# A query front that runs ahead of the first batch's attention, or mixed with it

## The chip, the cores and the metric

The kernel runs on one core of a Trainium2 chip. The metric is the device time of one execution in microseconds (us). A core has a matrix engine (TensorE, PE in the rows; its weight loads are PEld), VectorE (DVE), ScalarE (ACT), GpSimd (POOL) and SyncE (SP), which here only issues transfers (DMAs). Each takes its own list of instructions strictly in order; semaphores join the lists.

## The reference

Three residual blocks over 32 batches of 64 tokens of width 256: cross attention to 1601 context rows, span attention, and a feed-forward block with a shared expert and eight routed ones. Only the first matters here:

```python
def _L0_xattn_ref(q, k, v, mask, wq_w, wq_b, wk_w, wk_b, wv_w, wv_b, wo_w, wo_b):
    qh = _split_heads(q @ wq_w.T + wq_b)          # 16 heads of 16
    kh = _split_heads(k @ wk_w.T + wk_b)
    vh = _split_heads(v @ wv_w.T + wv_b)
    scores = jnp.einsum('bhqd,bhkd->bhqk', qh, kh) / jnp.sqrt(jnp.float32(D_K))
    scores = jnp.where(mask, scores, jnp.float32(-1000000000.0))
    attn = jax.nn.softmax(scores, axis=-1)
    out = jnp.einsum('bhqk,bhkd->bhqd', attn, vh)
    ...
    return out @ wo_w.T + wo_b
x = x + _L0_xattn_ref(_layernorm(x, axis=-1), ctx_1024, ctx_1024, mask, ...)
```

The mask of this case lets every row see every key.

## The kernel before

**Three parts.** `queries` normalizes x and projects the queries of all 2048 tokens, in four chunks of 512. `cross_attention` handles the 32 batches. `tail` is the second part, with span attention and experts; the change leaves it as it is.

**Queries.** A chunk passes: mean by matmul with 1/256 (M), subtraction (C), square (S), variance by matmul (V), ln and exp for the reciprocal deviation (I), the product with it (N, into `xn`), projection by `wq` (P), bias (B), clearing of dead rows (G), split into fp16 high and low parts (H, L). These parts are stored to a buffer in HBM, `q_parts`. `run_periods` sets the order: a period does one step of each kind, for chunks that lie one stage apart. The context of batch 0 is split into high and low parts there too (X, four chunks of 400 columns), and the masks, weights and biases are prepared.

**Between the parts.** `both` emits an engine's share of `queries`, then waits for all that was prepared (`ready`), then the share of `cross_attention`. On PE the latter begins with waits for the constant rows of the key stacks and for the ones in both value tiles, and then reads a register (`rows_all`) and branches: without masked rows it runs one unrolled copy of the loop, otherwise another.

**Cross attention.** A turn works on batch n and prepares batch n+1. In the letters of `SLOTS`: K (eight pieces) projects keys, six matmuls each, which ACT and DVE turn into `k_hi` and `k_lo`; V (thirteen) projects values; SP copies queries and keys into `qstack` and `kstack` (six transfers, and three for each of eight pairs of heads); M (32) is a score matmul whose maximum DVE takes; T turns the row maxima into rows of the query stack; S are the scores for the softmax, P the products with the values. H marks where POOL splits the next context but one into `ctx_hi` and `ctx_lo`; they have one buffer, so chunk i waits until the values of its rows are done. The turn that only prepares, `turn(-1)`, does batch 0's K, V, M and T after the queries.

Of the kernel before, what the change touches and what calls it, by code (L numbers as in the profile page):

```python
# [13 lines left out]
F32 = mybir.dt.float32  # L14
# [89 lines left out]
def build(nc, ins, out_dram):  # L104
    ctx = ExitStack()
    with ctx:
# [9 lines left out]
        wo_in = sem("wo_in")  # L116
# [4 lines left out]
        with ExitStack() as attention:  # L121
            def sb(name, shape, dt):
# [12 lines left out]
                kstack=[sb(f"kstack{i}", [P, PAIRS, S2P], F16) for i in range(2)],  # L135
# [3 lines left out]
                ctx_in=sem("ctx_in"),  # L139
                ctx_hi=sem("ctx_hi"),  # L140
                ctx_lo=sem("ctx_lo"),
                rows_in=sem("select_rows_in"), stack_zero=sem("stack_zero"),
            )
            before, ready = queries(nc, ins, bank, w, first_in, wo, bo, bo_all, wo_in, ident, mean_w, eps_col, q_parts, sem)
            cross = cross_attention(nc, sb, ins, bank, w, first_in, attn_out, out_done, q_parts, sem)
# [32 lines left out]
def run_periods(order, table):  # L178


    depth = max(late for late, _, _ in table.values())
    for period in range(NCH + depth):
        count = {}
        for step in order.split():
            late, do, arg = table[step]
            i = count.get(step, 0)
            count[step] = i + 1
            if 0 <= period - late < NCH:
                do(period - late, i if arg is None else arg)


def queries(nc, ins, bank, w, first_in, wo, bo, bo_all, wo_in, ident, mean_w, eps_col, q_parts, sem):
# [3 lines left out]
    with ExitStack() as own:  # L196
        def sb(name, shape, dt=F32):
# [4 lines left out]
        bq, bk_raw, bq_up = sb("bq", [P, NK]), sb("bk_raw", [P, NK]), sb("bq_up", [P, NK])  # L202
# [7 lines left out]
        sq = [sb(f"sq{i}", [P, NK, CW]) for i in range(2)]  # L210
        rstd = [sb(f"rstd{i}", [P, CW]) for i in range(2)]
        xn = [sb(f"xn{i}", [P, NK, CW]) for i in range(2)]
        q = [sb(f"q{i}", [P, NK, CW]) for i in range(2)]
        q_hi, q_lo = first_in["q_hi"], first_in["q_lo"]
        mean_bank, var_bank, proj_bank, row_bank, bias_bank = bank[0:2], bank[2:4], bank[4:6], bank[6], bank[7]

        x_in = [sem(f"q_x_in{c}") for c in range(NCH)]
        const_in, wq_in, w_in, mask_in = (sem("q_" + n) for n in ("const_in", "wq_in", "w_in", "mask_in"))
        memsets, up_done, parts_hi, consts, rows_seen, diag_ready, live_ready, live_done, bias_sum, bias_done = (
            sem("q_" + n) for n in ("memsets", "up_done", "parts_hi", "consts", "rows_seen", "diag_ready", "live_ready", "live_done",  # L220
                                    "bias_sum", "bias_done"))
        mean, xc_done, sq_done, var, lnv, rstd_done, xn_done, proj, biased, live, hi_done, lo_done = (
            sem("q_" + n) for n in "mean xc sq var lnv rstd xn proj biased live hi lo".split())
        q_out = [sem(f"q_out{i}") for i in range(2)]
        raw, c_hi, c_lo = first_in["raw"], first_in["c_hi"], first_in["c_lo"]

        PE_ORDER, DVE_ORDER, ACT_ORDER = "M V P", "C L N G X", "S H I B X"  # L230
# [4 lines left out]
        def sync(sp):  # L235
            def load(tile, src, done):
                sp.dma_start(tile, src).then_inc(done, 16)

            def rows(name):
                return ins[name].rearrange("(k p) n -> p k n", p=P)  # L240

            load(x[:, :, toks(0)], rows("xT")[:, :, toks(0)], x_in[0])
            load(wq[:], rows("wqT"), wq_in)
            load(bq[:], ins["bq"], wq_in)
            load(x[:, :, toks(1)], rows("xT")[:, :, toks(1)], x_in[1])
            load(ident[:], ins["c_ident"], const_in)
            for e in range(2):
                load(mask_u8[S * e:S * e + S, :], ins["maskQ"], mask_in)
            load(maskT_u8[:], ins["maskT"].rearrange("(n p) q -> p n q", p=P), mask_in)
            for c in range(2, NCH):  # L250
                load(x[:, :, toks(c)], rows("xT")[:, :, toks(c)], x_in[c])
# [4 lines left out]
            load(raw[:], ins["ctxT"][0].rearrange("(k p) s -> p k s", p=P), first_in["ctx_in"])  # L256
            for i in range(2):
                load(first_in["kstack"][i][KSTACK:KROWS, :, :], ins["c_select"].rearrange("r (p s) -> r p s", s=S2P), first_in["rows_in"])

            load(wo[:], rows("woT"), wo_in)  # L260
            load(bo[:], ins["bo"], wo_in)
            load(w["half_rows"][:], ins["c_half_rows"], wo_in)

            for c in range(NCH):
                sp.wait_ge(lo_done, c + 1)
                for i, part in enumerate((q_hi, q_lo)):
                    sp.dma_start(q_parts[i].rearrange("(k p) t -> p k t", p=P)[:, :, toks(c)], part[c % 2][:]).then_inc(q_out[c % 2], 16)
            for i in range(2):
                sp.wait_ge(q_out[i], 2 * 16 * (NCH // 2))

        def vector(dve):
            def centre(c, _):
                dve.wait_ge(x_in[c], 16)
                dve.wait_ge(mean, c + 1)

                need(dve, xn_done, c - 1)
                for k in range(NK):
                    i = nc.vector.tensor_tensor(xc[c % 2][:, k, :], x[:, k, toks(c)], mean_bank[c % 2][:, :], ALU.subtract)
                i.then_inc(xc_done, 1)

            def normalize(c, _):
                dve.wait_ge(rstd_done, c + 1)
                dve.wait_ge(xc_done, c + 1)

                need(dve, proj, c - 1)
                for k in range(NK):
                    i = nc.vector.tensor_tensor(xn[c % 2][:, k, :], xc[c % 2][:, k, :], rstd[c % 2][:], ALU.mult)
                i.then_inc(xn_done, 1)
                if c == 0:
                    mask_rows()  # L290
                if c == 1:
                    dve.wait_ge(live_ready, 1)
                    nc.vector.tensor_copy(row_live[:], row_bank[:, 0:S]).then_inc(live_done, 1)
                    nc.vector.tensor_copy(w["rows_all"][:], row_bank[0:1, S:S + 1]).then_inc(live_done, 1)
                    dve.wait_ge(live_done, 2)

            def clear(c, _):

                dve.wait_ge(biased, c + 1)
                for k in range(NK):  # L300
                    qv = q[c % 2][:, k, :].rearrange("p (b s) -> p b s", s=S)
                    i = nc.vector.tensor_tensor(qv, qv, row_live[:, :].unsqueeze(1).to_broadcast([P, CB, S]), ALU.mult)
                i.then_inc(live, 1)

            def low(c, _):
                dve.wait_ge(hi_done, c + 1)

                need(dve, q_out[c % 2], 2 * 16 * (c // 2))
                nc.vector.tensor_tensor(q_lo[c % 2][:], q[c % 2][:], q_hi[c % 2][:], ALU.subtract).then_inc(lo_done, 1)

            def split_lo(c, _):
                s0, n = CHUNKS[c]
                if c == 0:
                    weights_lo()
                for k in range(NK):
                    dve.wait_ge(first_in["ctx_hi"], NK * c + k + 1)
                    nc.vector.tensor_tensor(c_lo[:, k, s0:s0 + n], raw[:, k, s0:s0 + n], c_hi[:, k, s0:s0 + n].bitcast(F32),
                                            ALU.subtract).then_inc(first_in["ctx_lo"], 1)

            def weights_lo():  # L320

                dve.wait_ge(w_in, 4 * 16)
                dve.wait_ge(parts_hi, 2)
                nc.vector.scalar_tensor_tensor(w["wk_lo"][:], wk[:], UP, w["wk_hi"][:].bitcast(F32),
                                               ALU.mult, ALU.subtract).then_inc(consts, 1)
                nc.vector.tensor_tensor(w["wv_lo"][:], wv[:], w["wv_hi"][:].bitcast(F32), ALU.subtract).then_inc(consts, 1)
                nc.vector.tensor_scalar(w["bk"][:], bk_raw[:], UP, None, ALU.mult).then_inc(consts, 1)

            def mask_rows():

                dve.wait_ge(const_in, 16)
                dve.wait_ge(mask_in, 3 * 16)
# [4 lines left out]

            nc.vector.memset(mean_w[:], 1.0 / D).then_inc(memsets, 1)
            nc.vector.memset(eps_col[:], EPS).then_inc(memsets, 1)
            nc.vector.memset(ones_q[:], 1.0).then_inc(memsets, 1)  # L340
            for i in range(2):
                nc.vector.memset(first_in["qstack"][i][:], 0.0).then_inc(first_in["stack_zero"], 1)
# [1278 lines left out]
```

## Time and profile before

| | |
|---|---|
| median of 3 runs | 1549.67 us (1546.57 to 1555.34) |
| the profiled execution | 1546.79 us, span of its profile 1545.0 us |
| its granted TensorE clock, mean | 0.987 of full |
| busy share: PE, DVE, ACT, POOL | 95%, 65%, 60%, 28% |

"Span" is from the first to the last instruction. A row of the timeline has start, length, engine, line, operation, tiles and shape; what stands in brackets is the idle time before it and what ended it. Instructions may overlap on PE, so the step from start to start is what one costs.

### The profile page before, as it was taken

To read this page: it belongs to the slowest core of one execution; us is meant where nothing else is said; L and a number is where in the kernel's file an instruction comes from. 1 tells how busy PE (TensorE), PEld (TensorE's weight loads), DVE (VectorE), ACT (ScalarE), POOL (GpSimd) and SP (SyncE) were. 2 spreads that over 40 slices of the span, in tenths; PEclk is the share of its full clock that TensorE was granted. 3 is DMA by queue.
4 is the path that set the end of the run, shared out by engine and by line. 5 is a ranking of instruction groups with operands and counts; after the bars stand their busy time and mean duration, and the time that the engine had idled before them with its cause. 6 is when DMAs were issued, how large, how long until landed. Compare 5 with 4: busy or idle time off the path is not lost. (4 is left out here: it accounts for less than half of the span.)

```text
span 1545.0 us, 56243 instructions
## 1 busy us (share of the span) xinstructions
PE 1473.8 (95%) x23420; PEld 1243.0 (80%) x23420; DVE 1007.9 (65%) x3974; ACT 926.2 (60%) x1833; POOL 426.2 (28%) x549
## 2 busy tenths in 40 slices
PE   6699999999999999999999999999999997899899
PEld 2578888888888888888888888888888874466588
DVE  5666677767676766766667666666667654654445
ACT  4356566666666565666666566665666662597583
POOL 0133233333333333333333333333333301400043
PEclk9899999999999999999999999999999999899999
DMA  6444444444444444444444444443444313100012
GB/s 158 142 119 112 111 111 112 112 112 111 111 112 112 112 114 119 109 123 125 120 116 115 111 116 110 119 114 105 112 117 115 79 37 126 55 1 1 1 55 83
DMA packets 91759, 156.25 MB, mean 101 GB/s; under 512 B 44896, under 2 KB 55904, under 8 KB 91488
## 3 DMA queue, kind: packets, MB, share of 16 engines
q1 hardware_dynamic: 91216, 151.57, 36.9%
q8 instruction: 189, 3.10, 0.9%
q0 software_dynamic: 288, 1.05, 0.2%
q14 instruction: 66, 0.54, 0.1%
HBM read 69.61 MB, written 4.19 MB: 48 GB/s over the span
## 5 line engine op out<-in xcount | busy, mean ns | idle before, releaser
L663 DVE CUSTOM_DVE_ANT_0 junk<-bank,mask_q 128x400 bf16<-128x400 f32 (+1 forms) x1024 | 547.1, 571 | 180.1 <-issue 174.0
L615 ACT ACTIVATE probs<-bank 128x512 f32<-128x512 f32 (+1 forms) x832 | 467.5, 596 | 122.2 <-PE bank L788 113.1
L591 POOL CAST ctx_hi<-ctx_raw 128x400 fp32r<-128x400 f32 x248 | 122.1, 521 | 838.5 <-PE bank L752 838.5
L788 PE MATMUL bank<-qstack,kstack 104*128 104x128 f16 (+1 forms) x3328 | 289.8, 220 | 4.1 <-ACT probs L615 3.4
L752 PE MATMUL bank<-wv_hi,ctx_hi 128*128 128x256 f32 (+1 forms) x832 | 279.7, 336 | 0.2 <-issue 0.2
L769 PE MATMUL bank<-kstack,qstack 96*128 96x400 f16 (+1 forms) x1024 | 268.1, 336 | 5.7 <-issue 3.8
L654 DVE SCALAR_TENSOR_TENSOR k_lo<-bank,bk,k_hi 128x400 f16<-128x400 f32 (+1 forms) x256 | 162.3, 634 | 168.9 <-ACT k_hi L625 168.9
L635 ACT ACTIVATE v<-bank 128x256 f32<-128x256 f32 (+1 forms) x416 | 159.7, 384 | 184.2 <-PE bank L752 177.8
L788 PEld LDWEIGHTS bank<-qstack,kstack 104*128 104x128 f16 (+1 forms) x3328 | 213.9, 99 | 65.0 <-issue 16.7
L625 ACT ACTIVATE k_hi<-bank,bk 128x400 f16<-128x400 f32 (+1 forms) x256 | 152.4, 595 | 181.0 <-PE bank L742 172.9
L594 POOL TENSOR_TENSOR ctx_lo<-ctx_raw,ctx_hi 128x400 fp32r<-128x400 f32 x248 | 253.6, 1044 | 0.0
L752 PE MATMUL bank<-wv_lo,ctx_hi 128*128 128x256 f32 (+1 forms) x832 | 232.7, 280 | 0.0
L752 PE MATMUL bank<-wv_hi,ctx_lo 128*128 128x256 f32 (+1 forms) x832 | 232.4, 279 | 0.0
L803 PE MATMUL bank<-probs,v 128*32 128x64 f32 x13312 | 219.2, 221 | 6.4 <-issue 6.4
L803 PEld LDWEIGHTS bank<-probs,v 128*32 128x32 f32 x13312 | 197.6, 110 | 22.0 <-issue 14.3
L742 PE MATMUL bank<-ctx_hi,wk_hi 128*128 128x400 f32 (+1 forms) x512 | 190.6, 372 | 10.5 <-issue 10.0
L742 PE MATMUL bank<-ctx_hi,wk_lo 128*128 128x400 f32 (+1 forms) x512 | 178.6, 349 | 0.0
L742 PE MATMUL bank<-ctx_lo,wk_hi 128*128 128x400 f32 (+1 forms) x512 | 178.0, 348 | 0.2 <-issue 0.2
L752 PEld LDWEIGHTS bank<-wv_hi,ctx_hi 128*128 128x128 f32 (+1 forms) x832 | 154.4, 186 | 4.9
L752 PEld LDWEIGHTS bank<-wv_lo,ctx_hi 128*128 128x128 f32 (+1 forms) x832 | 154.6, 186 | 0.3 <-issue 0.3
L752 PEld LDWEIGHTS bank<-wv_hi,ctx_lo 128*128 128x128 f32 (+1 forms) x832 | 152.9, 184 | 0.0
L769 PEld LDWEIGHTS bank<-kstack,qstack 96*128 96x128 f16 x1024 | 82.1, 98 | 53.9 <-issue 19.1
(171 smaller groups left out, 1621.0 us busy)
## 6 DMA issues: line engine op xcount, KB each, us to landing
ctx_raw<-in_ctxT SPq DMA_DIRECT2D x32, 1602.0 KB, 6.9
kstack<-k_hi SPq DMA_DIRECT2D x512, 100.1 KB, 2.2
kstack<-k_lo SPq DMA_DIRECT2D x256, 100.1 KB, 2.2
weight<-in_w SPq DMA_DIRECT2D x18, 256.0 KB, 2.7
x<-in_xT SPq DMA_DIRECT2D x8, 512.0 KB, 6.4
qstack<-q_parts SPq DMA_DIRECT2D x192, 16.0 KB, 5.5
out_yT<-y SPq DMA_DIRECT2D x8, 256.0 KB, 3.3
weight<-in_sw SPq DMA_DIRECT2D x3, 512.0 KB, 6.4
```

What stands on the lines that cost most here:

```text
L591: nc.gpsimd.tensor_copy(c_hi[:, k, s0:s0 + n], raw[:, k, s0:s0 + n]).then_inc(ctx_hi, 1)
L594: nc.gpsimd.tensor_tensor(c_lo[:, k, s0:s0 + n], raw[:, k, s0:s0 + n], c_hi[:, k, s0:s0 + n].bitcast(F32), ALU.subtract).then_inc(ctx_lo, 1)
L615: nc.scalar.activation(probs[kt % NP][0:m, GROUPS * h:GROUPS * (h + 1), :], st[h][0:m, :], ACT.Exp, scale=DK ** -0.5 / (UP * UP)).then_inc ...
L625: nc.scalar.activation(k_hi[:, t, s0:s0 + n], pj[(b.slot + c) % 2][:, 0:n], ACT.Identity, bias=w["bk"][:, t:t + 1]).then_inc(khi_done, 1)
L635: nc.scalar.activation(heads, pj[(b.slot + NCK + i) % 2][0:m, 0:D].rearrange("s (p e d) -> s p e d", e=2, d=DK), ACT.Copy).then_inc(v_done, 1)
L654: nc.vector.scalar_tensor_tensor(k_lo[:, t, s0:s0 + n], pj[(b.slot + c) % 2][:, 0:n], w["bk"][:, t:t + 1], k_hi[:, t, s0:s0 + n], ALU.add, ...
L663: nc.vector.tensor_tensor_reduce(junk[i % SM][:, 0:n], sm[i % SM][:, 0:n], w["mask_q"][:, s0:s0 + n], 1.0, -3.0e38, ALU.add, ALU.max, part ...
L742: mm = nc.tensor.matmul(o, w[wp][:, k, t * P:(t + 1) * P], cp[:, k, s0:s0 + n], start=i == 0, stop=i == len(terms) - 1)
L752: mm = nc.tensor.matmul(o, cp[:, k, j * P:j * P + m], w[wp][:, k, :], start=i == 0, stop=i == len(terms) - 1)
L769: nc.tensor.matmul(sm[i % SM][:, 0:n], qstack[b.slot][0:KSTACK, p, :], kstack[b.slot][0:KSTACK, p, s0:s0 + n], start=True, stop=True).then ...
L788: mm = nc.tensor.matmul(st[h][0:m, g * PW:(g + 1) * PW], kstack[b.slot][0:KROWS, p, kt * P:kt * P + m], qstack[b.slot][0:KROWS, p, :], sta ...
L803: mm = nc.tensor.matmul(ob[32 * g:32 * g + 32, t * S:(t + 1) * S], v[b.slot][0:m, kt, c0:c0 + 2 * DK], probs[kt % NP][0:m, p, S * e:S * (e ...
```

## The change

The turn that prepares batch 0 and the query steps are written as one order for each engine, `FIRST_PE`, `FIRST_DVE`, `FIRST_ACT`, `FIRST_POOL` and `FIRST_SP`, emitted by `run_first`. Lower-case or new letters are query steps. The rest:

- The projection takes the centred x (`xc`), not `xn`. The deviation is multiplied in afterwards, from PSUM, and a second instruction adds the bias and clears dead rows (`finish`). ACT's bias step and DVE's normalizing step are gone.
- POOL, not DVE, computes `ctx_lo` for batch 0, the low parts of query chunks 1 to 3, the zeros of the query stacks and the ones of the values.
- `sq` has one buffer instead of two; the statistics and the projections have other banks of PSUM.
- The loads are issued in another order, and the context of batch 1 is loaded within the front (`c0`). The second buffers (`kstack1`, `v1`) share memory with the query part's tiles: their constant rows and ones are written at the end (`e0`, `o0`).
- The waits for all that is prepared are replaced by waits where each is first used. The register read and branch on PE stand behind T of batch 0.

```diff
-            before[name](eng)
-            for done, count in ready:
-                eng.wait_ge(done, count)
-            cross[name](eng)
+            cross[name](eng, before[name](eng))
...
+def run_first(order, table):
+    for step in order.split():
+        table[step[0]](int(step[1:]))
...
-            def normalize(c, _):
-                dve.wait_ge(rstd_done, c + 1)
...
-                    i = nc.vector.tensor_tensor(xn[c % 2][:, k, :], xc[c % 2][:, k, :], rstd[c % 2][:], ALU.mult)
...
+            def finish(c):
+                dve.wait_ge(proj, c + 1)
+                dve.wait_ge(rstd_done, c + 1)
...
+                    nc.vector.tensor_tensor(q[c % 2][:, k, :], proj_bank[k][:, :], rstd[c % 2][:], ALU.mult).then_inc(rescaled, 1)
...
+                    i = nc.vector.scalar_tensor_tensor(qv, qv, bq[:, k:k + 1], row_live[:, :].unsqueeze(1).to_broadcast([P, CB, S]),
+                                                       ALU.add, ALU.mult)
...
+            def low(c):
+                pool.wait_ge(hi_done, c + 1)
+
+                need(pool, q_out[c % 2], 2 * 16 * (c // 2))
+                nc.gpsimd.tensor_tensor(q_lo[c % 2][:], q[c % 2][:], q_hi[c % 2][:], ALU.subtract).then_inc(lo_done[c], 1)
...
-                need(act, var, c - 1)
-                nc.scalar.activation(sq[c % 2][:], xc[c % 2][:], ACT.Square).then_inc(sq_done, 1)
+                need(act, var, c)
+                nc.scalar.activation(sq[:], xc[c % 2][:], ACT.Square).then_inc(sq_done, 1)
...
+    FIRST_SP = "s0 Q0 D0 s1 D1 D2 D3 c0 s2 D4 D5 D6 D7 s3 e0 c1"
+    FIRST_POOL = "z0 X0 X1 X2 X3 a0 L1 L2 S0 S1 L3 S2 S3 o0"
...
+        def second_rows():
+
+            for c in range(NCH):
+                sp.wait_ge(lo_done[c], 1)
+            sp.dma_start(kstack[1][KSTACK:KROWS, :, :], ins["c_select"].rearrange("r (p s) -> r p s", s=S2P)).then_inc(d["rows_in"][1], 16)
+            for i in range(2):
+                sp.wait_ge(q_out[i], 2 * 16 * (NCH // 2))
...
-        for i in range(2):
-            ones = v[i][:].rearrange("s t (p j d) -> s (t p) j d", j=3, d=DK)[:, :, 1, :]
-            nc.vector.memset(ones, 1.0).then_inc(v_ones, 1)
...
-        pe.wait_ge(first_in["rows_in"], 2 * 16)
-        pe.wait_ge(v_ones, 2)
+        run_first(FIRST_PE, {**early, "K": lambda c: keys(at(0), c), "V": lambda j: values(at(0), j), "M": lambda i: chunk_scores(at(0), i),
+                             "T": lambda _: turn_shift(at(0))})
```

In the SP and POOL tables s stores a chunk of queries, Q and D fill the stacks, c loads a context, z and o write zeros and ones, X and S split contexts 0 and 1, a makes the masks, L a low part.

PE's list at the start of the program, before: all query matmuls (the lines up to L435), the bias matmul L446, the read of the register and the branch, and only then the first key projection (L742).

```order
L413 MATMUL bank<-x,mean_w 128x512 x4
L420 MATMUL bank<-sq,mean_w 128x512 x2
...
L435 MATMUL bank<-xn,wq 128x512 x8
L446 MATMUL bank<-bv,wo 128x1 x4
L836 TENSOR_LOAD rows_all
L836 ISA x2
L837 COMPARE_AND_BRANCH
L742 MATMUL bank<-ctx_hi,wk_hi 128x400
```

The same place now: means, the two small row matmuls, the projection of chunk 0 before its variance, and the first key piece (L755) ahead of the second projection (L419).

```order
L396 MATMUL bank<-x,mean_w 128x512 x4
L407 MATMUL bank<-row_diag,ones_q 128x64
L408 MATMUL bank<-ones_q,row_all 1x1
L419 MATMUL bank<-xc,wq 128x512 x4
L402 MATMUL bank<-sq,mean_w 128x512 x4
L396 MATMUL bank<-x,mean_w 128x512 x2
L755 MATMUL bank<-ctx_hi,wk_hi 128x400
...
L419 MATMUL bank<-xc,wq 128x512 x4
```

The row matmuls moved ahead of the first projection, and key pieces came between the query chunks.

PE's list where batch 0 is prepared and batch 1's keys begin, now. Before, the shift matmul (L775) was followed at once by L742.

```order
L765 MATMUL bank<-wv_hi,ctx_lo 65x256
L793 MATMUL bank<-turn_down,row_max 8x128
L858 TENSOR_LOAD rows_all
L858 ISA x2
L859 COMPARE_AND_BRANCH
L755 MATMUL bank<-ctx_hi,wk_hi 128x400
```

The read and the branch moved from behind the queries to this place; the copy for unmasked rows follows the branch directly.

POOL's list between the masks and the loop, now; before, it went from the masks (L354 to L358) directly to batch 1's split.

```order
L349 TENSOR_TENSOR q_lo<-q,q_hi 128x1024 x2
L590 CAST ctx_hi<-ctx_raw 128x400 x2
L593 TENSOR_TENSOR ctx_lo<-ctx_raw,ctx_hi 128x400 x2
L590 CAST ctx_hi<-ctx_raw 128x400 x2
L593 TENSOR_TENSOR ctx_lo<-ctx_raw,ctx_hi 128x400 x2
L349 TENSOR_TENSOR q_lo<-q,q_hi 128x1024
L590 CAST ctx_hi<-ctx_raw 128x400 x2
L593 TENSOR_TENSOR ctx_lo<-ctx_raw,ctx_hi 128x400 x2
L590 CAST ctx_hi<-ctx_raw 128x402 x2
L593 TENSOR_TENSOR ctx_lo<-ctx_raw,ctx_hi 128x402 x2
```

The low part of query chunk 3 (L349) came between the second and the third chunk of batch 1's split.

## Rows read from the trace of the kernel before

**Rows 1.** The page: busy time of the matrix engine over the span.

```profile
PE 1473.8 (95%) x23420; PEld 1243.0 (80%) x23420; DVE 1007.9 (65%) x3974; ACT 926.2 (60%) x1833; POOL 426.2 (28%) x549
```

**Rows 2.** Busy time by stretch: stretch, length, then PE, PEld, DVE, ACT, POOL, clock, DMA.

```profile
0.00:54.20 54.20, 31.80 (x76) 13.73 (x76) 33.58 (x53) 23.96 (x35) 3.07 (x8) 0.93 0.54 144
54.20:66.90 12.70, 12.11 (x48) 11.06 (x48) 4.07 (x7) 4.17 (x7) 0.00 (x0) 0.76 0.51 165
66.90:86.00 19.10, 16.88 (x113) 12.80 (x112) 17.58 (x99) 5.59 (x14) 9.79 (x14) 1.00 0.46 107
```

**Rows 3.** The same view, the stretch after PE's long gap.

```profile
54.00:60.00 6.00, 5.73 (x17) 5.65 (x18) 1.27 (x2) 1.19 (x2) 0.00 (x0) 0.50 0.76 274
```

**Rows 4.** Timeline of PE, the query part.

```profile
5.99 5.20 PE L413 MATMUL bank<-x,mean_w 128*128 128x512 f32 x8 [5.99 <-DMA bq<-in_bq]
...
20.58 0.43 PE L425 MATMUL bank<-row_diag,ones_q 64*128 64x64 f32 x2 [3.07 <-DVE row_diag L336]
...
24.60 1.88 PE L413 MATMUL bank<-x,mean_w 128*128 128x512 f32 x4
26.32 1.88 PE L420 MATMUL bank<-sq,mean_w 128*128 128x512 f32 x4
28.03 3.60 PE L435 MATMUL bank<-xn,wq 128*128 128x512 f32 x8
...
44.22 0.95 PE L446 MATMUL bank<-bv,wo 128*128 128x1 f32 x8
54.27 0.69 PE L742 MATMUL bank<-ctx_hi,wk_hi 128*128 128x400 f32 x1 [9.11 <-issue]
```

**Rows 5.** Timeline of PE, keys, then values with maxima.

```profile
60.09 0.43 PE L742 MATMUL bank<-ctx_lo,wk_hi 128*128 128x400 f32 x1
...
61.88 0.45 PE L742 MATMUL bank<-ctx_hi,wk_hi 128*128 128x400 f32 x1 [0.26 <-DVE k_lo L654]
...
64.00 0.34 PE L742 MATMUL bank<-ctx_lo,wk_hi 128*128 128x400 f32 x1
...
71.38 0.42 PE L752 MATMUL bank<-wv_hi,ctx_hi 128*128 128x256 f32 x1
...
72.61 0.42 PE L752 MATMUL bank<-wv_hi,ctx_hi 128*128 128x256 f32 x1
```

**Rows 6.** Timeline of DVE: row reduction, a query step, the ones.

```profile
16.71 1.81 DVE L333 TENSOR_REDUCE row_all<-mask_u 64x1 f32<-64x1601 uint8 x1
...
26.17 1.29 DVE L302 TENSOR_TENSOR q<-q,row_live 128x512 f32<-128x512 f32 x2 [0.61 <-ACT q L381]
...
51.68 1.45 DVE L718 MEMSET v<- 128x1664 f32 x1 [0.30 <-issue]
```

**Rows 7.** Groups of 54 to 86 us: busy us, mean ns, then idle before.

```profile
L663 DVE CUSTOM_DVE_ANT_0 junk<-bank,mask_q 128x400 bf16<-128x400 f32 x24 | 12.7, 571 | 0.2 <-issue 0.2
```

**Rows 8.** Transfers of the first 90 us: count, size, median us from issue to landing.

```profile
x<-in_xT SPq DMA_DIRECT2D x4, 512.0 KB, 6.1
...
q_parts<-q_lo SPq DMA_DIRECT2D x4, 256.0 KB, 2.5
...
qstack<-q_parts SPq DMA_DIRECT2D x9, 16.0 KB, 6.1
```

**Rows 9.** The context tile's three transfers of the first 110 us.

```profile
DMA to landing us min/median/max: 7.0/7.4/12.3
```

**Rows 10.** Timeline, all engines, where batch 1 begins.

```profile
85.14 0.99 POOL L591 CAST ctx_hi<-ctx_raw 128x402 fp32r<-128x402 f32 x2 [1.51 <-PE bank L752]
...
86.01 0.45 PE L742 MATMUL bank<-ctx_hi,wk_hi 128*128 128x400 f32 x1
86.08 2.06 POOL L594 TENSOR_TENSOR ctx_lo<-ctx_raw,ctx_hi 128x402 fp32r<-128x402 f32 x2
...
88.17 0.40 SPq L549 DMA_DIRECT2D ctx_raw<-in_ctxT  x1
...
97.53 0.67 PE L769 MATMUL bank<-kstack,qstack 96*128 96x400 f16 x3 [0.69 <-issue]
```

More of the change, by code:

```diff
@@ L175, in build, with queries @@
         tail(nc, ins, bank, attn_out, out_done, wo, bo_all, mean_w, eps_col, ident, out_dram, sem)
[L178 to L192, printed above, removed]
+def run_first(order, table):
+    for step in order.split():
+        table[step[0]](int(step[1:]))
+def queries(nc, ins, bank, w, first_in, d, wo, bo, bo_all, ident, mean_w, eps_col, q_parts, sem):
     with ExitStack() as own:
@@ L268, in sync @@
-            for i in range(2):
-                sp.wait_ge(q_out[i], 2 * 16 * (NCH // 2))
+            load(raw[:], ins["ctxT"][0].rearrange("(k p) s -> p k s", p=P), d["ctx_in"])
+            for c in range(2, NCH):
+                load(x[:, :, toks(c)], rows("xT")[:, :, toks(c)], x_in[c])
+            load(mask_u8[S:2 * S, :], ins["maskQ"], mask_in)
+            load(maskT_u8[:], ins["maskT"].rearrange("(n p) q -> p n q", p=P), mask_in)
+            load(wo[:], rows("woT"), d["wo_in"])
+            load(bo[:], ins["bo"], d["wo_in"])
@@ L372, in inverse, with high @@
                 act.wait_ge(lnv, c + 1)
                 nc.scalar.activation(rstd[c % 2][:], rstd[c % 2][:], ACT.Exp, scale=-0.5).then_inc(rstd_done, 1)
[L375 to L384 removed]
+            def high(c):
@@ L436, in project @@
                                              start=k == 0, stop=k == NK - 1)
                 i.then_inc(proj, 1)
-            pe.wait_ge(memsets, 3)
-            pe.wait_ge(wq_in, 2 * 16)
-            run_periods(PE_ORDER, {"M": (0, means, None), "V": (1, variances, None), "P": (2, project, None)})
-            pe.wait_ge(wo_in, 3 * 16)
-            pe.wait_ge(w_in, 4 * 16)
-            for m in range(NK):
-                for k in range(NK):
-                    i = nc.tensor.matmul(bias_bank[:, m:m + 1], wo[:, k, m * P:(m + 1) * P], w["bv"][:, k:k + 1],
-                                         start=m == 0 and k == 0, stop=k == NK - 1, skip_group_check=True)
@@ L646, in turn, with vector @@
                         values(nxt, i)
+        run_first(FIRST_ACT, {**early, "K": lambda c: keys_hi(at(0), c), "V": lambda i: values(at(0), i)})
+        for c in range(NCH):
+            act.wait_ge(lo_done[c], 1)
         turns(act, turn)
-    def vector(dve):
+    def vector(dve, early):
         def keys_lo(b, c):
@@ L660, in chunk_max @@
             dve.wait_ge(sm_ready, NMX * b.n + i + 1)
+            if first(b) and i == 0:
+                dve.wait_ge(d["masks"], 4)
             nc.vector.memset(lead[:, i:i + 1], 0.0)
@@ L737, in keys @@
                 pe.wait_ge(ctx_lo, SPLIT * b.n + NK * (c + 1))
+            if first(b) and c == 0:
+                pe.wait_ge(d["weights_lo"], 3)
             piece_free(b, c)
```

318 lines of the change are left out of this document (163 added, 155 removed).

## The prediction

> **What bounds the kernel now.** I read the page first: PE is busy for 95% of the span [rows 1], so whatever PE stands still for, or does at half clock, is time of the kernel. Then busy time by stretch [rows 2]: from 0 to 54.2 us, while the queries are made, PE works 31.8 us and DVE 33.6; neither is full. From 54.2 to 66.9 (batch 0's keys) PE is full, but at a mean clock of 0.76; from 54 to 60 us it was granted 0.50 [rows 3], the lower of its two levels, 1.2 GHz. From 66.9 to 86.0 (values and maxima) DVE leads with 17.6 of 19.1 us: 24 maxima cost 12.7 us, 0.53 each [rows 7]. Then the timeline of PE. It waits until 5.99 for the first loads, 3.07 us for the row reduction, and 9.11 us at 54.27 [rows 4]: its last query matmul was long over, and it stood behind the queries' tail on the other engines and the writing of ones, which DVE ended at 51.68 + 1.45 = 53.13 [rows 6]. Batch 1's first key matmul starts at 86.01 [rows 10]; from there on PE is busy nearly without a break and the code is the same in both kernels. So the question is when that matmul starts, and what the new front leaves late behind it.
>
> **PE's work in the new front.** The steps from start to start give the prices: a mean or a variance 26.32 - 24.60 = 1.72, a projection 3.5 (3.60 with its tail), the bias matmuls 0.95 [rows 4]. Two key pieces take 64.00 - 61.88 + 0.18 = 2.30, so one 1.15; a value piece with three score matmuls takes 72.61 - 71.38 = 1.23 [rows 5]. At the lower clock 18 key matmuls took 60.09 - 54.27 = 5.8 us [rows 4, 5], twice the full-clock price.
>
> The first projection cannot start before chunk 0 is centred. That now stands behind the row reduction: mask and identity are the second and third loads; from the 6.1 us of a load of x [rows 8] and a start near 1.5 I estimate 7.5 for their arrival. Then 3.8 us for two reductions of 1.8 and the diagonal [rows 6], 1.25 for the centring (two passes, like the 1.29 of a query step [rows 6]): the projection starts at 12.7. Before, it came at 21.1, so this chain is shorter although the centring itself is 2 us later.
>
> From 12.7 PE has: 4 projections 14.0, 4 variances and means of chunks 2 and 3 10.3, bias 1.0, 8 key pieces 9.2, and 13 value pieces with 32 score matmuls 15.2 (ten groups of 1.23 and 2.9 for the rest). Sum 49.7.
>
> **What PE still waits for.** Following each order through the semaphores I find three waits:
> - The square of chunk 1 must wait for the variance of chunk 0, as there is one `sq`: 1.1 us.
> - The query chain. Variance 0 ends at 17.8; then ACT does square 1, one context chunk, ln and exp (3.3 us), DVE finishes the chunk with four passes (2.6, twice the 1.29 of [rows 6]), ACT is still at two context chunks and the next ln and exp (0.6), high part 1.0, low part 1.2, two stores 0.4 apart that land 2.5 after issue [rows 8], the first query load 0.5 behind, the last of six 3.1 later, landing 6.1 after issue [rows 8]. That is 17.8 + 3.3 + 2.6 + 0.6 + 1.0 + 1.2 + 2.9 + 0.5 + 3.1 + 6.1 = 39.1, with a handover 39.3. PE reaches the first score matmul at 38.5: 0.8 us of waiting.
> - The last maximum and the reduction over them, before the shift matmul: 0.8 us.
>
> Sum 2.7. Key transfers are covered: pairs 0 to 3 are ready when the queries are; pair 4 leaves at some 50.8 and is wanted at 55. DVE has 45 us of work between 7.5 and 65 (maxima 17, finish 10, keys 5, centring 5, reductions 4, the rest 4), close behind PE but not ahead. POOL's larger share is hidden in its idle time (3.07 of the first 54 us busy [rows 2]); ACT loses work.
>
> T ends at 12.7 + 49.7 + 2.7 + 0.3 = 65.4. Behind it now stands the read of the register and the branch. Before, it lay in the gap: from the ones' end at 53.13 to the key matmul at 54.27, 1.14 us [rows 4, 6]. Nothing is below it there but that read, so I take 1.1 (bounds 0.5 and 3.6, below). Keys of batch 1 start at 66.5 instead of 86.01: **19.5 us earlier**. The half-clock stretch, 2.9 us of loss, is within that sum, since PE never stands still for more than some 1.1 us.
>
> The Trainium skill, "Runtime: NRT & Kernel Launch", section "Instruction fetch mechanics", says that a taken branch breaks the sequential fetch of instructions and forces a fetch of the target. By that rule this place could cost more than before, as the branch stands at another point of the code.
>
> **What is late behind it.** Batch 1's context is split by POOL behind the values of batch 0. Before, POOL ended at 88.14 and the next context load left at 88.17, 2.16 us after PE's 86.01 [rows 10]; six query loads follow it on SP, and the first score matmul of batch 1 at 97.53 already waited 0.69 us for them. Now POOL's list has a low part of a query chunk between the split chunks. A split chunk is 3.0 (0.99 + 2.06 [rows 10]); the low part has no row on POOL: from 2.06/2 for 400 columns it is 2.65 for 1024; its bounds are DVE's price, 1.3, and twice POOL's, 5.3. From the fourth value piece at some 54.8: 3.1 + 3.0 + 2.65 + 3.0 + 3.0 = 69.6. The load leaves 3.1 us after the keys' start at 66.5, not 2.16. **1.0 us is given back** at that score matmul. The key piece that needs the last split chunk starts 4.1 us after the keys' start, as before, at 70.6: just covered; with 5.3 it is not, and 2.7 more is lost. The constant rows of `kstack1` are a load in front of this context; issued with the last query store near 64, I take them as over (bounds 0 and 3).
>
> Net: 19.5 - 1.0 = 18.5. Against the profiled execution, 1546.8 - 18.5 = 1528.3. The median of the runs is 2.9 above it and one run 8.5, so I add 1.7 and say **1530**.
>
> **Rivals.**
> - *The start is late.* Context chunk 0 on ACT stands in front of ln and exp. Its load took 12.3 us from issue, against 7.4 later on [rows 9], since it was issued behind nearly all others. Now it is issued near 6 and I expect it at 16 or 17; wanted at 18.9. If it comes at 21, or the last query load lands later than 6.1, the first score matmul shifts by as much: each us costs one. With that, a POOL low part of 5.3 and a slow row load, 5 to 10 us are lost: 1533 to 1540. For it: each such time is from one execution, and the chain has no slack. Against it: fewer bytes stand in front of each of these loads. Chance 0.17.
> - *The branch costs a fetch.* The shortest transfer among the rows, 2.5 us from issue to landing [rows 8], can be set in for it: branch 3.6, time 1532.5. For it: the code before it is longer than in the old kernel. Against it: the unmasked copy follows directly, and the old stretch had the same instructions for 1.14. This is the skill's rule; the old trace gives it at most 1.14. Chance 0.04.
> - *The mixing blocks itself.* In-order lists with steps of two chains: a step that waits holds back one of the other chain, and DVE, nearly full, ends the front at 77 us or later. Then less than 8 us remain: 1539 to 1548. For it: 45 us of DVE work must fit to PE's order. Against: before, PE had 22 us of standing still in the first 54 [rows 2], and the chain to the first score matmul ends at 39. Chance 0.05.
> - *Slower: PE stays at 1.2 GHz through the front.* Work at half clock costs twice [rows 3 to 5]. The 18.5 us are gone once 18.5 us of full-clock work, of the 49.7, run at the lower level; if all did, +30: 1560. For it: PE was at the lower level for 6 us after standing still. Against: after its wait of 3.07 us the steps are still 1.72 [rows 4], and the planned waits are shorter. Chance 0.02.
> - *The waits are not there*, loads land a us earlier and the groups overlap better: T at 61 to 62, time 1524 to 1526. Chance 0.05.
>
> **How the numbers follow.** My forecast has 0.67; its own range, by the single bounds (start -1 and +2, POOL -1 and +2.7, rows 3, durations 1), is 1526 to 1535. The range reaches into the first rival and the last: 1524 to 1539. What a measurement of this kernel can tell from no change is about 0.5%, 7.7 us. Faster by more: all but the blocked mixing and the slow clock, 0.93. Within: 0.05. Slower: 0.02.
>
> **What would show it.** Right: first projection near 12.7, first score matmul near 39 with a wait under 2 us, T near 65, a gap of 1.1 behind it, POOL's last split chunk at 69 to 70, a wait of 1 to 2 us at batch 1's first score matmul, clock 1.00 in every stretch up to 86. Wrong: PE idle for more than 3 us in sum after 12.7, or a key or score matmul of batch 1 that waits longer than before.

## The result, and the profile after

| | before | after |
|---|---|---|
| median of 4 runs, us | 1550.02 (1546.57 to 1555.34) | 1530.00 (1528.68 to 1535.25) |
| profiled execution, us (span) | 1546.79 (1545.0) | 1530.81 (1528.6) |

The ratio is 0.9868, with a 95% interval of 0.9846 to 0.9890: faster by 20 us (1.3%), as forecast (1530). The profiled pair alone stands 16.0 us apart, since the profiled execution of before lies 3.2 us under its median and that of after 0.8 above. The page's line of the engines, to be held against [rows 1]: PE does the same work (1470 against 1474 us) in a shorter span.

```profile
PE 1470.1 (96%) x23420; PEld 1241.6 (81%) x23420; DVE 999.5 (65%) x3958; ACT 921.0 (60%) x1825; POOL 447.8 (29%) x564
```

Busy time by stretch, the stretches of [rows 2]: in the first 54.2 us PE now works 45.9 us where it worked 31.8, and no stretch is below full clock.

```profile
0.00:54.20 54.20, 45.88 (x154) 25.82 (x155) 35.30 (x87) 22.68 (x35) 20.55 (x21) 1.00 0.63 186
54.20:66.90 12.70, 11.15 (x86) 9.72 (x84) 12.19 (x58) 5.45 (x13) 11.12 (x13) 1.00 0.59 143
66.90:86.00 19.10, 16.87 (x238) 15.11 (x239) 8.58 (x29) 9.48 (x19) 4.70 (x6) 1.00 0.64 176
```

The timeline of PE: the first projection, every wait over 0.4 us from there to batch 1's first score matmul, and batch 0's first score matmul at 40.58, which does not wait. A row is start, length, engine, line, operation, tiles, and in brackets the idle time ahead of it.

```profile
12.31 3.70 PE L419 MATMUL bank<-xc,wq 128*128 128x512 f32 x8
...
18.93 1.98 PE L402 MATMUL bank<-sq,mean_w 128*128 128x512 f32 x4 [1.21 <-ACT sq L358]
...
32.63 0.42 PE L755 MATMUL bank<-ctx_hi,wk_hi 128*128 128x400 f32 x1 [1.86 <-DVE k_lo L663]
...
40.58 0.68 PE L785 MATMUL bank<-kstack,qstack 96*128 96x400 f16 x3
...
65.43 0.39 PE L793 MATMUL bank<-turn_down,row_max 128*8 128x128 f32 x2 [0.52 <-DVE row_max L681]
66.85 0.42 PE L755 MATMUL bank<-ctx_hi,wk_hi 128*128 128x400 f32 x1 [1.03 <-POOL ctx_lo L593]
...
79.89 0.67 PE L785 MATMUL bank<-kstack,qstack 96*128 96x400 f16 x3 [2.23 <-DMA qstack<-q_parts]
```

DVE: the start of the row reduction and of the centring, and the passes that finish a query chunk. The second pass (L281) of chunks 0 and 1 takes 2.20 and 3.27 us while POOL works, that of chunks 2 and 3 takes 1.41. The first pass (L277) of chunk 1 has POOL beside it too and takes 1.28, as with POOL idle (1.29 at 38.55).

```profile
5.97 1.81 DVE L301 TENSOR_REDUCE row_all<-mask_u 64x1 f32<-64x1601 uint8 x1 [4.84 <-DMA ident<-in_c_ident]
...
9.71 1.27 DVE L263 TENSOR_TENSOR xc<-x,bank 128x512 f32<-128x512 f32 x2
...
22.38 2.20 DVE L281 SCALAR_TENSOR_TENSOR q<-q,bq,row_live 128x512 f32<-128x512 f32 x2
...
27.48 1.28 DVE L277 TENSOR_TENSOR q<-bank,rstd 128x512 f32<-128x512 f32 x2
28.68 3.27 DVE L281 SCALAR_TENSOR_TENSOR q<-q,bq,row_live 128x512 f32<-128x512 f32 x2
...
39.76 1.41 DVE L281 SCALAR_TENSOR_TENSOR q<-q,bq,row_live 128x512 f32<-128x512 f32 x2
```

POOL: the masks beside that pass, the low part of query chunk 3, and the last split chunk of batch 1's context. Behind that, SP issues the context load of batch 2 at 70.25 and batch 1's six query loads from 70.68.

```profile
29.44 1.97 POOL L332 TENSOR_SCALAR mask_q<-mask_u 128x1601 bf16<-128x1601 uint8 x1
31.38 1.30 POOL L333 TENSOR_SCALAR mask_k<-maskT_u 128x832 bf16<-128x832 uint8 x1
...
62.16 2.15 POOL L349 TENSOR_TENSOR q_lo<-q,q_hi 128x1024 f16<-128x1024 f32 x1
...
68.11 2.06 POOL L593 TENSOR_TENSOR ctx_lo<-ctx_raw,ctx_hi 128x402 fp32r<-128x402 f32 x2
```

SP: the six query loads of batch 0, and the two issues behind POOL.

```profile
30.48 2.70 SPq L552 DMA_DIRECT2D qstack<-q_parts  x6
...
70.25 0.38 SPq L540 DMA_DIRECT2D ctx_raw<-in_ctxT  x1
70.68 3.42 SPq L552 DMA_DIRECT2D qstack<-q_parts  x6
```

The view of `qstack` gives their time from issue to landing, first for 29 to 36 us, then for 70 to 76 us:

```profile
DMA to landing us min/median/max: 1.7/1.7/1.8
DMA to landing us min/median/max: 5.2/5.7/6.1
```

Batch 1's keys start 19.2 us earlier than in [rows 10], its first score matmul 17.6 earlier. From there on the profile of after adds nothing: from the second shift matmul (after 104.4, before 122.0) the two kernels stand 17.6 apart, at the last one (1239.3 and 1256.5) 17.2. Over the 14 profiled executions of this study the stretch from the third shift matmul to the last took 1093 to 1100 us, whatever the front was, so single executions differ by some us with no cause in the front. The head varies too: in the eleven other executions whose head was left as it is, the first projection starts between 11.24 and 13.81 us.

### The profile page after: what moved, and what is told of

Its sections match the earlier page's. It is cut to its first block and busy times, and to the rows that moved or that the text cites. A ratio compares the mean times of both kernels' runs of the same rounds, so it can differ in the third digit from the quotient of the medians.

```text
span 1528.6 us, 56227 instructions
## 1 busy us (share of the span) xinstructions
PE 1470.1 (96%) x23420; PEld 1241.6 (81%) x23420; DVE 999.5 (65%) x3958; ACT 921.0 (60%) x1825; POOL 447.8 (29%) x564
## 3 DMA queue, kind: packets, MB, share of 16 engines
q0 software_dynamic: 288, 1.05, 0.2%
## 5 line engine op out<-in xcount | busy, mean ns | idle before, releaser
L755 PE MATMUL bank<-ctx_hi,wk_hi 128*128 128x400 f32 (+1 forms) x512 | 190.4, 372 | 3.7 <-DVE k_lo L663 2.1
L755 PE MATMUL bank<-ctx_lo,wk_hi 128*128 128x400 f32 (+1 forms) x512 | 176.4, 345 | 0.7 <-issue 0.7
L755 PE MATMUL bank<-ctx_hi,wk_lo 128*128 128x400 f32 (+1 forms) x512 | 176.9, 346 | 0.0
L785 PEld LDWEIGHTS bank<-kstack,qstack 96*128 96x128 f16 x1024 | 81.9, 98 | 51.2 <-issue 16.5
```

Source lines behind the costliest of these rows:

```text
L755: mm = nc.tensor.matmul(o, w[wp][:, k, t * P:(t + 1) * P], cp[:, k, s0:s0 + n], start=i == 0, stop=i == len(terms) - 1)
L785: nc.tensor.matmul(sm[i % SM][:, 0:n], qstack[b.slot][0:KSTACK, p, :], kstack[b.slot][0:KSTACK, p, s0:s0 + n], start=True, stop=True).then ...
```

## The experiments

Every kernel is the changed one with the edit shown; its idle times are read from the timeline of PE. Medians and ratios come from runs on the same chip as runs of the kernel before.

**1. The front without the mixing.** The orders are written out one chain after the other; helpers and operations are the same.

```diff
-    FIRST_PE = """m0 m1 R0 p0 v0 v1 m2 K0 p1 K1 v2 B0 K2 K3 p2 ...
+    FIRST_PE = """m0 m1 R0 p0 v0 v1 m2 p1 v2 p2 m3 v3 p3 B0 K0 K1 ... K7 M0 M1 ... T0"""
     (ACT, DVE, POOL and SP likewise: queries, then keys, then maxima and values)
```

> The changed kernel with its five orders unmixed: all query steps first, then batch 0's keys, then values and maxima; every other edit stays (rescaling after the projection, waits at first use, POOL's share, the early query loads). Theory A (the gain is PE work laid into the query chain's gaps): PE stands still for some 8 us more, the shift matmul of batch 0 comes at 71 to 75 us instead of 65.4, so of the 20 us gained at this point 11 to 14 come from the removed barrier, the ones, and the half clock, and 6 to 9 from the mixing. Theory B (the barrier and the clock are the whole gain): the shift matmul is within 2 us of 65.4.

Measured: 1543.35 us, 6 below the kernel before on that chip (1549.32). The shift matmul starts at 82.27, batch 1's keys at 83.38. PE's timeline has three waits that after does not have:

```profile
37.71 2.40 PE L402 MATMUL bank<-sq,mean_w 128*128 128x512 f32 x4 [2.52 <-ACT sq L358]
...
49.86 0.42 PE L753 MATMUL bank<-ctx_hi,wk_hi 128*128 128x400 f32 x1 [1.93 <-DVE k_lo L661]
...
70.66 0.51 PE L783 MATMUL bank<-kstack,qstack 96*128 96x400 f16 x1 [3.56 <-DMA kstack<-k_hi]
```

Of the 19.2 us at batch 1's keys, the other edits give 2.6 (86.01 to 83.38) and the mixed orders 16.5 (83.38 to 66.85). One shift matmul later (118.55, against 121.98 before and 104.38 after) the shares are 3.4 and 14.2. My number for the unmixed front was too good by far: it also runs at half clock after these waits (granted 0.68 at 40 to 44 us, 0.50 at 72 to 76).

Not all of the 16.5 is work laid into gaps. The last wait is for key-stack loads that SP issues right behind the context load of batch 1:

```profile
61.28 0.59 SPq L538 DMA_DIRECT2D ctx_raw<-in_ctxT  x1
```

The key-stack loads issued from 50 to 60 us land 2.2 us after issue, those from 60 to 64 us in 6.5 to 7.5. This wait of 3.56 us and the half clock behind it (4 x (0.27 + 0.50 + 0.09) = 3.4, from the windows 68 to 80) make 7 us, which another order of SP alone might avoid; no run tried it. So the mixing on the compute engines is worth some 9.5 to 16.5 us here, by one execution of each front.

**2. Batch 1's query loads early.** They are issued inside the front instead of behind the context load of batch 2.

```diff
-    FIRST_SP = "s0 Q0 D0 s1 D1 D2 D3 c0 s2 D4 D5 D6 D7 s3 e0 c1"
+    FIRST_SP = "s0 Q0 D0 s1 D1 D2 D3 c0 s2 Q1 D4 D5 D6 D7 s3 e0 c1"
```

> Batch 1's six query loads are issued within the front, behind the third query store, instead of behind the context load of batch 2. Theory A (at batch 1's first score matmul PE waits for the query loads, because the context load in front of them leaves late): the wait of 2.23 us at 79.89 us goes, and all later turns are 1.5 to 2.2 us earlier (last shift matmul near 1237). Rival: the key stack loads, issued from 74.15 on, are the real limit and land at nearly the same time; the wait keeps more than 1.5 us.

Measured: 1525.35 us; batch 1's first score matmul starts at 78.22 with no wait, though its keys started 0.5 later (67.33) than in after. So the 2.23 us were the query loads. When timed again below, 1.02 us of a wait stood there.

**3. The register read early.** PE reads `rows_all` between variances 0 and 1; behind the shift matmul only the branch is left.

```diff
+            def read_rows(_):
+                pe.wait_ge(d["live_done"], 2)
+                first_in["rows_all"] = pe.value_load(w["rows_all"][0:1, 0:1], min_val=0, max_val=S)
...
-        rows_all = pe.value_load(w["rows_all"][0:1, 0:1], min_val=0, max_val=S)
+        rows_all = first_in["rows_all"]
```

> The register with the number of live rows is read early on PE (between the first variance and the second); only the compare and branch stay behind the shift matmul. Theory A (the 1.1 us between the shift matmul and batch 1's first key matmul are the read of the register): that gap falls to 0.1 to 0.3 us, and the read hides in the 1.2 us that PE waits for the square of chunk 1. Rival (the branch itself, or a fetch behind it, costs it): the gap stays above 0.8 us.

Measured: 1529.82 us. The gap behind the shift matmul is gone:

```profile
68.37 0.39 PE L797 MATMUL bank<-turn_down,row_max 128*8 128x128 f32 x2 [0.53 <-DVE row_max L685]
68.69 0.45 PE L759 MATMUL bank<-ctx_hi,wk_hi 128*128 128x400 f32 x1
```

In after the profile put that 1.03 down to POOL's `ctx_lo`; with the read moved the same semaphores are waited for and nothing is left. The same holds in every run of this study: 0.84 to 1.05 us in the six executions of a mixed front with the read behind the shift matmul, no gap in the six with it moved. So the gap was the read, and the branch cost nothing that shows. The shift matmul itself is later here: means 0 and 1 took 3.75 and 3.78 us with a wait between, and the clock was at 0.74 from 32 to 36 us (see 5).

**4. Masks behind the low part of query chunk 1 on POOL.**

```diff
-    FIRST_POOL = "z0 X0 X1 X2 X3 a0 L1 L2 S0 S1 L3 S2 S3 o0"
+    FIRST_POOL = "z0 X0 X1 X2 X3 L1 a0 L2 S0 S1 L3 S2 S3 o0"
```

> On POOL the masks are made behind the low part of query chunk 1 instead of ahead of it. Theory A (DVE's second finishing pass took 3.27 us for chunk 1, against 1.41 for chunks 2 and 3, because POOL worked beside it): beside the masks it no longer stretches, the pass falls to 1.4 to 2.2 us, PE's wait of 1.86 us at 32.63 falls under 1, and the shift matmul comes 0.7 to 1.5 us earlier. Rival (the pass is long for another reason, such as operands in other memory banks or PSUM traffic): it stays at 3.2 us.

Measured: 1529.14 us. In the timelines of DVE, PE and POOL, the second pass of chunk 1 falls from 3.27 to 2.00 us, and the masks, now not beside it, from 1.97 and 1.30 to 1.53 and 0.87:

```profile
28.32 2.00 DVE L281 SCALAR_TENSOR_TENSOR q<-q,bq,row_live 128x512 f32<-128x512 f32 x2
...
31.02 0.42 PE L755 MATMUL bank<-ctx_hi,wk_hi 128*128 128x400 f32 x1 [0.62 <-DVE k_lo L663]
...
33.61 1.53 POOL L332 TENSOR_SCALAR mask_q<-mask_u 128x1601 bf16<-128x1601 uint8 x1
```

The pass still has POOL's `ctx_lo` beside its first 0.8 us. PE's wait for `k_lo` is 0.62 instead of 1.86, and the shift matmul comes at 63.85, 1.6 earlier; 0.35 of that is a head that started earlier (first projection at 11.96), the other 1.23 the wait. But the time is only 1.7 below after's, and the second shift matmul starts at 104.4 as in after. Behind a wait of 2.30 us at batch 1's first score matmul the clock was 0.60 from 80 to 84 us (windows of that kernel); in after it was 1.00:

```profile
80.00:84.00 4.00, 4.00 (x134) 3.68 (x134) 0.34 (x2) 0.78 (x2) 0.00 (x0) 0.60 0.43 100
```

**5. After again, and the early query loads, in five rounds.**

> The changed kernel again, unaltered, as the yardstick for the two kernels timed beside it. Both theories: median 1528 to 1533 us, ratio to the kernel before 0.985 to 0.989; first shift matmul near 65.4, wait of about 2.2 us at batch 1's first score matmul.

> The kernel with batch 1's query loads issued in the front, timed now in five rounds (its one look gave 1525.35 us with no wait at batch 1's first score matmul). Theory A (those loads behind the context load are the largest part of what is given back): median 4 to 6 us below the changed kernel beside it. Theory B (the single look was a lucky execution, and the wait moves to another place in the turns): within 2 us of it.

Measured: after 1532.04 us (1527.29 to 1533.28), ratio 0.9872 [0.9852, 0.9891]; early query loads 1528.28 (1527.43 to 1533.29), ratio 0.9856 [0.9835, 0.9877]. The 3.8 us lie between the two theories, and the intervals overlap, so the gain is likely but not shown. In the profiled execution of the early loads, batch 1's first score matmul waits 1.02 us, for nothing that the profile names. Both profiled executions have a half-clock stretch that the first profile of after had not; the windows of after, run again:

```profile
32.00:36.00 4.00, 3.89 (x14) 3.38 (x15) 1.34 (x4) 2.79 (x5) 2.77 (x4) 0.70 0.11 18
36.00:40.00 4.00, 4.00 (x12) 2.02 (x11) 0.85 (x2) 0.00 (x0) 0.00 (x0) 0.87 0.43 114
...
80.00:84.00 4.00, 2.77 (x16) 2.37 (x17) 1.66 (x10) 1.09 (x2) 0.00 (x0) 0.68 0.70 172
84.00:88.00 4.00, 4.00 (x142) 3.50 (x141) 0.78 (x5) 0.77 (x2) 0.00 (x0) 0.90 0.61 138
```

They lie behind the wait for `k_lo` (1.88 us, ending at 32.11) and the wait at batch 1's first score matmul (2.45, ending at 81.23). Each is estimated to lose 1.7 us of full clock: 4 x (0.30 + 0.13) and 4 x (0.32 + 0.10). From the `k_lo` wait's end to the shift matmul it is 34.42 us here and 32.80 in after.

**6. Chunk 0 centred before the row reduction.**

```diff
-    FIRST_DVE = """r0 C0 w0 C1 l0 ...
-    FIRST_PE = """m0 m1 R0 p0 v0 v1 ...
+    FIRST_DVE = """C0 r0 w0 C1 l0 ...
+    FIRST_PE = """m0 m1 p0 R0 v0 v1 ...
```

> Chunk 0 is centred before the row reduction on DVE, and PE does the first projection before the matmuls of the row reduction. Theory A (the head is set by the chain that reduction, centring, projection make): projection starts at 10.5 instead of 12.31, first shift matmul at 63.5 to 64.3, time 1527 to 1529 us. Theory B (the head's bound is the chain of squares, variances and inverses on ACT, whose context chunk 0 lands near 16 to 18 and stands ahead of the first ln): the projection is earlier, but the wait at variance 1 grows by about as much, first shift matmul at 65 to 66, time 1530 to 1531.

Measured: 1530.23 us, with the wait at variance 1 unchanged (1.21). The projection starts at 10.95, 1.36 before that of after, and the key piece behind the `k_lo` wait at 31.84, 0.79 before: now variance 0 stands behind the row reduction. But other executions with the old head and the masks in their old place have that key piece at 31.95 and 32.11 (experiment 5), so a gain of 0.1 to 0.8 us is no more than the spread. The clock was 0.64 at 32 to 36 us, and the shift matmul came at 66.28, 34.44 us behind the key piece, 1.64 more than in after. Theory B's time is right, and its reason fits: against the early query loads of experiment 5 the projection starts 0.68 earlier (11.63 there), variance 1 only 0.11 (18.14 against 18.25). That this edit gains anything is not shown.

**7. All three edits (2, 3 and 4), on two chips.**

> All three edits at once: batch 1's query loads early, the register read early on PE, the masks moved on POOL behind the low parts of the first query chunks. Theory A (the three losses are separate waits on one chain and add): first shift matmul at 64 to 65, batch 1's keys 0.3 behind it, its first score matmul at 75 to 76 without a wait, median 6 to 9 us below the changed kernel. Theory B (PE was ahead at the head but something behind it, POOL's split of batch 1's context or DVE's maxima, now sets the pace): score matmul at 77 or later with waits on ctx_lo or part_max over 1 us in sum, median 3 to 5 us below, no better than the early query loads alone.

> The kernel with the three edits (query loads early, register read early, masks later) once more, as the yardstick for the two kernels beside it. Median 1525 to 1529 us; batch 1's keys near 63.7, an idle stretch of 1 to 2.5 us before its first score matmul near 76 to 77.

> A look at the same kernel once more, for the spread of the idle stretch before batch 1's first score matmul: 1 to 2.5 us, with the first key-stack loads landing 4 to 5 us after issue.

Measured: 1526.87 us (1526.20 to 1532.15), ratio 0.9841 [0.9823, 0.9860]; on the second chip 1525.07 (1524.63 to 1526.67), ratio 0.9838 [0.9825, 0.9852]; one more execution there 1530.20. The shift matmul is at 63.4 to 64.0, the keys 0.3 behind it. But batch 1's first score matmul waits 2.40, 1.55 and 2.00 us, and the profile names nobody. Theory A had the shift matmul and the keys right, but not the score matmul without a wait; the median is 5.2 us below that of after beside it, under A's 6 to 9 and over B's 3 to 5. Against the early query loads alone it is 1.4 us, within the noise. PE and SP in the first of them:

```profile
77.14 1.01 PE L790 MATMUL bank<-kstack,qstack 96*128 96x400 f16 x3 [2.40 <-issue]
```

```profile
67.88 0.38 SPq L544 DMA_DIRECT2D ctx_raw<-in_ctxT  x1
70.56 0.52 SPq L563 DMA_DIRECT2D kstack<-k_hi  x1
71.12 0.59 SPq L563 DMA_DIRECT2D kstack<-k_lo  x1
71.77 0.58 SPq L563 DMA_DIRECT2D kstack<-k_hi  x1
```

The view of `kstack` in that stretch says how long these three took from issue to landing:

```profile
DMA to landing us min/median/max: 4.4/4.4/5.3
```

71.77 + 5.3 = 77.1, the start of the matmul: the first key-stack loads (100 KB each) are late next, issued 2.7 us behind a context load of 1602 KB.

**8. The context load behind the key-stack loads of pairs 0 to 3.**

```diff
-    FIRST_SP = "... e0 c1"
+    FIRST_SP = "... e0"
                 for p in range(PAIRS):
                     lay_out_pair(nxt, p)
+                    if isinstance(nxt.n, int) and nxt.n == 1 and p == 3:
+                        load(at(2))
```

> The three edits, and the context load of batch 2 is issued behind the key-stack loads of pairs 0 to 3 of batch 1 instead of before them. Theory A (PE now waits for the first key-stack loads, which share the DMA engines with the 1602 KB of the context load that left 2.7 us before them): those loads land 2.3 to 3 us after issue, batch 1's first score matmul at 74.6 to 75.3 with 0 to 0.6 us of waiting, median 1 to 2.5 us below the kernel with three edits. Theory B (the wait is for something else, since the profile names no releaser: the low part of the last key piece or a bank): the wait stays at 2 us or more, time within 1 us of it; then the later context load also costs nothing, as its first reader starts at 86.

Measured: 1529.42 us (1527.26 to 1530.67), ratio 0.9859 [0.9843, 0.9875]. The loads now land as fast as said, and the score matmul at 75.38 does not wait:

```profile
DMA to landing us min/median/max: 2.1/2.2/2.2
```

Theory A has its mechanism. Its time is wrong: the load meets the later key-stack loads instead, which take 6.3 to 8.5 us to land, and PE waits 3.01 us at 90.03, the clock falling behind it:

```profile
90.03 0.51 PE L792 MATMUL bank<-kstack,qstack 96*128 96x400 f16 x1 [3.01 <-DMA kstack<-k_hi]
```

```profile
88.00:92.00 4.00, 1.97 (x11) 1.79 (x11) 0.58 (x3) 0.60 (x1) 3.04 (x5) 0.60 0.81 195
92.00:96.00 4.00, 4.00 (x108) 3.30 (x107) 1.16 (x6) 1.47 (x3) 2.84 (x4) 0.55 0.02 7
```

That is an estimated 3.0 + 4 x (0.40 + 0.45) = 6.4 us lost for the 2 saved; the median is 4.4 us above that of the three edits on the same chip (1525.07). "Costs nothing, as its first reader starts at 86" looked at the reader and forgot the loads that share the DMA engines with it.

**9. Query chunk 3's low part on DVE** instead of POOL, beside the three edits.

```diff
-    FIRST_POOL = "z0 X0 X1 X2 X3 L1 a0 L2 S0 S1 L3 S2 S3 o0"
+    FIRST_POOL = "z0 X0 X1 X2 X3 L1 a0 L2 S0 S1 S2 S3 o0"
-        M16 M17 M18 ...
+        L3 M16 M17 M18 ...
```

> The three edits, and the low part of query chunk 3 is made by DVE ahead of maximum 16 instead of by POOL between the split chunks of batch 1's context. Theory A (the context load leaves when POOL's split ends, 2.1 us earlier, so that most of it is over when the key-stack loads leave): context load at 65.8 to 66.5, first score matmul of batch 1 with less than 1 us of waiting; DVE's extra 1.2 us delays the first shift matmul by 0 to 1.2, so the median is 0 to 2 us below the kernel with three edits. Theory B (DVE sets the end of the front): shift matmul 1 us or more later than 63.4 and the wait at batch 1 unchanged, time 0 to 2 us above it.

Measured: 1527.35 us (1525.94 to 1529.27), ratio 0.9849 [0.9835, 0.9863]. DVE stands waiting for the high part (0.84 us) and then takes 1.58, so PE waits for a maximum and the shift matmul comes at 67.47, 3.4 to 4.1 later than in the three profiles with three edits:

```profile
58.07 0.52 PE L790 MATMUL bank<-kstack,qstack 96*128 96x401 f16 x1 [1.61 <-DVE part_max L679]
```

The clock fell behind that wait:

```profile
56.00:60.00 4.00, 2.39 (x12) 1.84 (x11) 3.52 (x13) 0.48 (x2) 2.47 (x3) 0.72 0.79 213
60.00:64.00 4.00, 4.00 (x27) 3.63 (x26) 3.26 (x20) 1.29 (x4) 3.12 (x5) 0.86 0.44 95
```

The delay is the wait of 1.61, an estimated 1.7 of clock, and 0.53 for a key-stack load at 55.06. Batch 1's first score matmul does not wait and starts at 78.50, against 76.62 to 77.37 with three edits, so about half of the loss or more is made good. Theory B for the delay, A for the wait; the median is 2.3 us above 1525.07, with overlapping intervals.

## Why the prediction was right, step by step

**The start.** Forecast: reduction at 7.5, projection at 12.7. The reduction began at 5.97, and projection 0 at 12.31. Of the 1.5 us by which the reduction was early, only 0.4 came through, because PE was still at its two means (8 matmuls from 5.25, 6.65 us) and then at the matmuls of the reduction, which begin at 11.83.

**PE's work.** Forecast 49.7. From 12.31 to the shift matmul at 65.43 are 53.12 us; without the waits of 1.21, 1.86 and 0.52 that is 49.5.

**The waits.** Forecast 1.1, 0.8 and 0.8, in sum 2.7; measured 1.21, none, and 0.52, and one that I had not seen, 1.86 for `k_lo`: 3.6. The query chain was mis-sized: the six loads, issued from 30.48 over 2.70 us, landed 1.7 us after issue and not 6.1 [rows 8], so the queries were there near 34.9, where I had said 39.1, and PE came at 40.6. The missed wait comes from a price: I took the finishing of a chunk at twice 1.29 us. Its second pass takes 2.20 and 3.27 beside POOL, and `k_lo` stands behind it in DVE's list. Moving the masks away (4) takes 1.24 off the wait, and in the six executions with the masks moved the wait is 0.60 to 0.62, against 1.86 to 1.89 in the six without, so this is shown. That the shift matmul fits is in part luck: forecast was a start at 65.1 (its end at 65.4), measured 65.43 (end 65.82), with 0.4 too much for the head, 0.2 for PE's work, 0.8 and 0.3 for two of the waits, and 1.86 missing for a fourth.

**The read and the branch.** Forecast 1.1; 1.03 measured, and experiment 3 shows that it is the read. The rival of a branch that costs a fetch is out for this place: keys follow the shift matmul by 0.32 us when only the branch is between. The Trainium skill, "Runtime: NRT & Kernel Launch", section "Instruction fetch mechanics", has a taken branch force a fetch when its target lies outside the two pages of instructions that are held, a condition that the prediction left out. The copy for unmasked rows follows this branch directly, so the case is no test of that rule; no gap is left that the trace shows.

**POOL and what is late behind it.** Forecast: low part 2.65, last split chunk ending at 69.6, the load 3.1 us behind the keys' start. Measured: 2.15, 70.17, and 70.25 - 66.85 = 3.40. The term "1.0 us is given back" was too small: the wait is 2.23 against 0.69, so 1.5 is given back; in the run of 5 it is 1.8 (2.45 against 0.69), and an estimated 1.7 more to the clock. Experiment 2 takes the wait away in one execution and leaves 1.02 in another.

**Rivals.** A late start did not show, nor did the mixing block itself: at the end PE waits only 0.52 us for DVE's last maxima. That the mixed orders carry the gain, not the shorter chain alone, is shown by experiment 1, with the reserve on SP's order said there. The slower rival, half clock, is partly true: not in the profile of after, but in that of the same kernel run again, where two stretches cost an estimated 3.4 us. The sentence that PE never stands still for more than some 1.1 us was wrong.

**The signs of being wrong.** The prediction named two, and both came true: PE is idle for 1.21 + 1.86 + 0.52 = 3.6 us between 12.31 and the shift matmul, and 1.03 more behind it, where "more than 3 us in sum" was the sign; and batch 1's first score matmul waits 2.23 us against 0.69 before. They were badly chosen, since the forecast itself had 2.7 + 1.1 = 3.8 us of idle time and 1 us more at that matmul. They show what the time does not: the waits were worse than thought, and the earlier head and the faster landing of the query loads made up for it.

**The sum.** Net gain 18.5 at batch 1's first score matmul was forecast, 17.6 measured in the profiled pair, of which 16.4 is left over the whole span; the medians differ by 20.0 and, when timed again, by 18.8. The 1.7 added because the profiled execution of before lies under its median had the right direction; that the median came out at 1530.00 to the tenth is luck.

**A better kernel.** Query loads early, read early, masks later: 1525.07 us on one chip and 1526.87 on another, where after took 1532.04. On that chip four of the better kernel's five executions (1526.2 to 1527.4) lie over 3 us below five of after's six (1530.95 to 1533.28), but the 95% intervals of the ratios, 0.9823 to 0.9860 and 0.9852 to 0.9891, overlap slightly: better is likely, by how much is open.

## What to carry to other kernels

Count a front by the engine that must not stand still, and price each filler by what runs beside it; a pass beside POOL took up to 2.3 times its price alone. Once a wait is filled, ask which transfer leaves next and what large load shares the DMA engines with it: here the place of the wait went from the query loads to the first key-stack loads to the later ones. A gain of 1 to 2 us in one stage is settled only by a profile of that stage, and by more than one execution of it.

## What the runs showed of the hardware

- The same wait costs differently. Behind the `k_lo` wait of 1.86 to 1.89 us (six executions) the granted clock fell in four of them, to 0.63 to 0.74 over 32 to 36 us, and stayed at 1.00 in two. Behind the wait of 0.60 to 0.62 at that place (six executions) it never fell there. At batch 1's first score matmul it fell behind waits of 2.00, 2.09, 2.30, 2.40 and 2.45 us, not behind 2.23 and 2.78, nor behind 1.02 and 1.55. Elsewhere it fell behind 1.61 (9), 2.52 and 3.56 (1) and 3.01 (8), not behind 1.93 (1) or behind the 3.07 of before [rows 4].
- DVE and POOL can slow each other. DVE's second pass takes 1.41 us with POOL idle, 2.00 to 2.20 beside POOL's `ctx_lo`, 3.27 beside the masks; the masks take 1.97 and 1.30 us beside it, 1.53 and 0.87 elsewhere. Not every pass does: the first one, which reads its operand `bank` from PSUM, takes 1.27 to 1.29 either way, and the second pass of chunk 3 keeps its 1.41 with POOL's cast beside part of it. Which property decides is not shown.
- Loads of 100 KB into the key stack land in 2.1 to 2.2 us when no large load is under way, in 4.4 to 5.3 when issued 2.7 us behind 1602 KB, and in 6.3 to 8.5 when issued shortly ahead of and behind it, from 76 to 84 us in 8.
- What stays open: turns 3, 15 and 27 are 1 to 3.5 us longer than the others in nearly all profiles; no run was aimed at it.
